# A phase mixer with a ternary feed-forward layer: the context's statistics behind the first of four product units, their spread behind the second, and a new first step

## The chip, the cores and the metric

The kernel runs on one core of one Trainium2 chip. The metric is the device time of one execution in microseconds, the median of several runs. The times before are 1537.38, 1531.16 and 1529.48 us.

## The reference

The input x has 16 sequences of 1024 positions with 256 features, in fp32.

```
h   = layernorm(x)
omega = h @ W_omega.T + b_omega
phi = cumsum(omega * exp(log_scale) / sqrt(position))
cm_real, cm_imag = h * cos(phi), h * sin(phi)
mem_real, mem_imag = cumsum(cm_real) / position, cumsum(cm_imag) / position
ret_real = mem_real * cos(phi) + mem_imag * sin(phi)
ret_imag = mem_imag * cos(phi) - mem_real * sin(phi)
context = concat(cm_real, cm_imag, ret_real, ret_imag)        # 1024 features
g   = gelu((layernorm(context) * gamma + beta) @ W1.T + b1)   # 512
x1  = x + h + g @ W2.T + b2
out = x1 + relu(layernorm(x1) @ T(F1).T + f_b1) @ T(F2).T + f_b2
```


## The kernel before

**Tiling.** The 16384 rows are 32 chunks of 512; two chunks make a sequence, and the second takes up the first one's sums by carries (`carry_phase`, `carry_imag`, `carry_real`). Features lie on the 128 partitions. Every product is made in fp16 from a high and a low part: `context_hi` on ScalarE writes the high part `ch`, `context_lo` on VectorE the difference `cl`, and so for the gelu's output (`gelu_hi`, `gelu_lo`), the relu's (`relu_hi`, `relu_lo`) and the two norms.

**Steps.** Each engine has a `step(s)`, run for s from -1 to 31, whose order is written out by hand. In one step four chunks are under way: `now` (s) is in its feed-forward layer, `nxt` (s+1) in the two mixer products, `ahead` (s+2) in phase, sums and context, `far` (s+3) in its first norm and omega; `before` (s-1) is stored. Engines meet by semaphores alone; a wait stands in front of the instruction that needs it, and all behind it on that engine wait too. In step -1 there is no `now`; in that step the weights for later products are turned too.

**TensorE** (L1033). `hidden(nxt, m)` (L955) for m from 0 to 3 is one of four product units: 24 matmuls of 512 columns into bank 4+m. `context_stats(nxt)` (L930) sums the context over its features with 72 one-column matmuls into bank 3, 64 from `ch` and `cl`, 8 from the sums of squares `q_hi` and `q_lo`. `spread(nxt)` (L949) turns the reciprocal deviations `crs` into a row on all partitions, in bank 2. The order is unit 0, unit 1, statistics, unit 2, spread, unit 3. Then come eight `ffn_in` (L970) into banks 4 to 7, with `omega(far)` (L915) behind the sixth, `ffn_out` (L991) three behind them into banks 0 and 1, and `mixer_out(nxt)` (L1005), the product with w2, into banks 4 and 5; then the last three `ffn_out`. In step -1 the groups of the second weight (`W2_GROUPS`, `turn_group`, `less_hi`) and the signs of the feed-forward weights (`SIGN_GROUPS`, `turn_signs`, L1102) are turned between the units: two groups ahead of the spread, the other six behind unit 3 and ahead of omega and `mixer_out`. Each group is copied out of its bank by ScalarE's `group_hi` (L831); two banks serve in turn. `ffn_in(0, 0)` waits for all of them.

**VectorE** (L1431). `fraction(ahead)`, `statistics_1(far)`, `lean_2(now)`, `modulate_imag(ahead)` (L1259), `sums_imag`, `gains_1(far)`, `modulate_real`, carry, `context_variance(nxt)` (L1335: five small instructions from bank 3 to `cve`), `second_lo(now)` (L1389), `memory_imag`, `sums_real`, `scale_hidden(nxt, 0..2)` (L1352: a unit times the spread row `rb`, out of its bank to z), `first_rows_lo(far)`, then the retrieval, `scale_hidden(nxt, 3)`, low parts and `relu_lo` among one another, `phase_turns(far)` (L1222), `mixer_residual(nxt)` (L1364), `phase_sums(far)` (L1232: two scans of 512), `statistics_2(nxt)`, `spread_2(nxt)`.

**ScalarE** (L737). `sums_hi(nxt)` (L654), `base_scaled(ahead)`, `whole_turns(ahead)`, `output(before)`, `sine`, `magnitude`, `normalise_2(now)`, `cosine`, `second_hi(now)`, `normalise_1(far)`, `modulated_hi(ahead)`, `first_rows_hi(far)`, `spread_out(nxt)` (L663: bank 2 to rb), three gelus, and the relus with the squares (`square_real`, `square_imag`) and casts of the retrieved parts among them.

**POOL** (L509). `base_bias(ahead)`, `inverse_std_2(now)` (L500, ve2 to rs2), `square_lo(nxt)` (L539), `inverse_std_1(far)` (L476), `x1_bias(now)`, `inverse_std_context(nxt)` (L504, cve to crs), `product_imag_sin(ahead)`, `retrieve(ahead)` (two accumulating DMAs, rr and ri), `output_sum(before)` (an accumulating DMA to the output), `square_sums(ahead)` (L531): behind `sqr_done`, `sqi_done` and `cl_done[3]` an addition of 1024 columns (L535), then one of 512 (L537). SyncE's queue transposes the norms' rows by DMA (turned2 for `ffn_in`, turned1 for omega), loads x and stores the output.

Of the kernel before, what the change touches and what calls it, by code (L numbers as in the profile page):

```python
# [43 lines left out]
def phase_mixer_layer(nc, x, w_omega, b_omega, log_scale, ln_gamma, ln_beta, w1, b1, w2, b2,  # L44
# [17 lines left out]
    with ctx:  # L62
# [140 lines left out]
        ps_rows_b = ps[:, 4:6, :].rearrange("p b (t d) -> p (b t) d", d=D)  # L203
        ps_rows_last = ps[:, 2:4, :].rearrange("p b (t d) -> p (b t) d", d=D)
# [137 lines left out]
        def need_sum(eng, s, c, back=0):  # L342

            wait(eng, s, c.counts.value(16, 16 * (c.more + 1 - back)))

# [121 lines left out]
        def _(pool):  # L467
# [41 lines left out]
            def step(s):  # L509
                before, now, nxt, ahead, far = s.chunk(-1), s.chunk(0), s.chunk(1), s.chunk(2), s.chunk(3)  # L510
                if ahead:
                    base_bias(ahead)
                if now:
                    inverse_std_2(now)
                if nxt:
                    square_lo(nxt, ahead)
                if far:
                    inverse_std_1(far)
                if now:
                    x1_bias(now)  # L520
                if nxt:
                    inverse_std_context(nxt)
                if ahead:
                    product_imag_sin(ahead)
                    retrieve(ahead)
                if before:
                    output_sum(before)
                if ahead:
                    square_sums(ahead)

            def square_sums(c):  # L531
                need(pool, sqr_done, c)
                need(pool, sqi_done, c)
                need(pool, cl_done[3], c)
                pool.tensor_tensor(sqr[:, :, :], sqr[:, :, :], turn[:, :, :], ALU.add).then_inc(q2_done, 1)  # L535
                need(pool, q2_done, c)
                pool.tensor_tensor(sqr[:, 0], sqr[:, 0], sqr[:, 1], ALU.add).then_inc(q_done, 1)  # L537

            def square_lo(c, after):  # L539
                if after:  # L540
                    need(pool, frac_done, after)
                need(pool, q_done, c)
                need(pool, qh_done, c)
                pool.tensor_tensor(q_lo, sqr[:, 0], q_hi, ALU.subtract).then_inc(ql_done, 1)
# [23 lines left out]
        def _(act):  # L568
# [36 lines left out]
            def whole_turns(c):  # L605
                need(act, y_done, c)
                need(act, q2_done, c, 1)
                act.activation(turn[:, :, :], ph[:, :, :], ACT.Identity, bias=rounder[:, 0:1]).then_inc(turn_done, 1)
# [128 lines left out]
            def step(s):  # L737
# [10 lines left out]
                if not now:  # L748
                    whole_turns(ahead)
                if nxt:  # L750
                    sums_hi(nxt)
# [18 lines left out]
                if now:  # L770
                    second_hi(now)
                if far:
                    normalise_1(far)
                if ahead:
                    modulated_hi(ahead)
                if far:
                    first_rows_hi(far)
                if nxt:
                    spread_out(nxt)
# [10 lines left out]
                if nxt and not now:  # L790
# [4 lines left out]
                    for n in SIGN_GROUPS[4:]:  # L795
                        group_hi(n)
# [104 lines left out]
            prepared(act)  # L901
# [3 lines left out]
        def _(pe):  # L905
# [49 lines left out]
            def hidden(c, m):  # L955
                if m < 2:
# [48 lines left out]
            def mixer_out(c, before):  # L1005
# [11 lines left out]
                rows = ps_rows_last if c.index == CHUNKS - 1 else ps_rows_b  # L1017
# [15 lines left out]
            def step(s):  # L1033
                now, nxt, ahead, far = s.chunk(0), s.chunk(1), s.chunk(2), s.chunk(3)
                if nxt:
                    hidden(nxt, 0)
                    if not now:
                        for n in W2_GROUPS:
                            turn_group(n)
                    hidden(nxt, 1)  # L1040
                    context_stats(nxt, ahead)
# [3 lines left out]
                if nxt:  # L1045
# [103 lines left out]
            prepared(pe)  # L1149
# [3 lines left out]
        def _(dve):  # L1153
# [210 lines left out]
            def mixer_residual(c):  # L1364
# [3 lines left out]
                dve.scalar_tensor_tensor(out=x1[:, c.b], in0=ps_rows_last if c.index == CHUNKS - 1 else ps_rows_b,  # L1368
# [62 lines left out]
            def step(s):  # L1431
# [18 lines left out]
                if ahead:  # L1450
                    modulate_imag(ahead)
                    sums_imag(ahead)
# [5 lines left out]
                if nxt:  # L1458
# [10 lines left out]
                if nxt:  # L1469
                    scale_hidden(nxt, 0)  # L1470
                    scale_hidden(nxt, 1)
                    scale_hidden(nxt, 2)
# [40 lines left out]
                if far:  # L1513
# [12 lines left out]
                if nxt:  # L1526
                    mixer_residual(nxt)
                if far:
# [107 lines left out]
            first_lo(second)  # L1636
            dve.wait_ge(p_spread, 3)
# [14 lines left out]
            context_lo(first, 1, cmi[:, :, :])  # L1652
            context_lo(first, 2, rr[:, :, :])
            context_lo(first, 3, ri[:, :, :])
            phase_turns(second)
            phase_sums(second)
            carry_phase(second)
# [31 lines left out]
```

## Time and profile before

| | |
|---|---|
| median of 3 runs | 1531.16 us (1529.48 to 1537.38) |
| profiled execution: its time | 1533.96 us |
| profiled execution: span | 1532.2 us |
| mean granted TensorE clock | 0.991 |
| TensorE matmuls busy | 1470.5 us, 96% |
| VectorE busy | 1438.2 us, 94% |
| ScalarE busy | 1253.4 us, 82% |
| POOL busy | 616.9 us, 40% |
| accumulating DMAs' queue (q0) | 83.37 MB, 34.3% of 16 engines |
| SyncE's and ScalarE's queue (q1) | 69.25 MB, 18.4% |

The span runs from the first to the last instruction. Busy is the union of an engine's instructions; issuing a DMA, waiting and registers don't count. A row of a timeline has its start, its length, the engine, the line of the kernel, the operation, output and inputs, the count of merged instructions and in brackets the idle time ahead with what ended it. Times are from the start of the span.

### The profile page before, as it was taken

The page shows a single profiled execution, that of the slowest core. Times are in us where ns is not written, and L with a number is a line of the kernel's source. Part 1 is how long each engine was busy: PE and PEld are TensorE (multiplying, and loading weights), DVE is VectorE, ACT ScalarE, POOL GpSimd, SP SyncE. Part 2 cuts the span into 40 slices and gives each one's busy share as a digit, 9 for nine tenths or more (in the row PEclk, how much of TensorE's full clock was granted, in tenths as well). Part 3 has the DMA queues.
Part 4 walks back from the last instruction along what each step waited for, and adds up shares of the span by engine and source line. Part 5 has one row for each costly group of instructions (what it writes and reads, how often), then busy time and mean ns, then how long its engine had stood idle before and what let it go on. Part 6 is the DMA issues. An engine that isn't in the chain of part 4 may idle for free.

```text
span 1532.2 us, 29929 instructions
## 1 busy us (share of the span) xinstructions
PE 1470.5 (96%) x10685; PEld 878.0 (57%) x10685; DVE 1438.2 (94%) x2325; ACT 1253.4 (82%) x1773; POOL 616.9 (40%) x393
## 2 busy tenths in 40 slices
PE   3779999999999999999999999999999999999998
PEld 2445566656555665555665655566565566555556
DVE  7999999999999999999999999999999999989954
ACT  6768888888988888988888898888888788888756
POOL 1333444433354443444444334444344444334331
PEclk9899999999999999999999999999999999999999
DMA  6325545555645655654555564455565455555452
GB/s 219 67 58 111 102 80 109 108 111 113 123 76 100 111 104 111 124 107 79 105 111 110 111 125 94 83 111 103 109 125 109 73 109 111 110 111 101 73 90 42
DMA packets 231427, 158.20 MB, mean 103 GB/s; under 512 B 138608, under 2 KB 221552, under 8 KB 231280
## 3 DMA queue, kind: packets, MB, share of 16 engines
q0 software_dynamic: 59376, 83.37, 34.3%
q1 hardware_dynamic: 170272, 69.25, 18.4%
q10 hardware_dynamic: 1632, 3.67, 0.7%
q8 instruction: 86, 1.41, 0.4%
q14 instruction: 61, 0.50, 0.1%
HBM read 24.13 MB, written 33.03 MB: 37 GB/s over the span
## 4 chain that ended last, share of the span: by engine, by line
DVE 35%; PE 24%; issue 14%; ACT 12%; POOL 7%; DMA 4%; SPq 2%; DVEq 1%; ACTq 0%; POOLq 0%
PE ps L966 11%; DVE arena L1332 5%; POOL sqr L535 4%; DVE arena L1400 4%; PE ps L1000 4%; PE ps L987 4%; POOL sqr L537 3%; PE ps L1021 3%; ACT xs L601 3%; DVE mr L1285 3%; ACT base L581 3%; DVE arena L1361 2%; DVE bn L1170 2%; DVE arena L1356 2%; DVE qb L1316 2%
## 5 line engine op out<-in xcount | busy, mean ns | idle before, releaser
L966 PE MATMUL ps<-arena,w_hi 128*128 128x512 f16 x2048 | 609.2, 379 | 3.0 <-DVE arena L1332 1.6
L966 PE MATMUL ps<-arena,w_lo 128*128 128x512 f16 x1024 | 388.3, 379 | 0.0
L966 PEld LDWEIGHTS ps<-arena,w_hi 128*128 128x128 f16 x2048 | 197.5, 98 | 224.2 <-issue 2.0
L987 PE MATMUL ps<-turned,fw_t 128*128 128x512 f16 x1024 | 250.6, 380 | 8.6 <-DMA turned<-rows 4.1
L1000 PE MATMUL ps<-fw_t,arena 128*128 128x256 f16 x2048 | 255.0, 273 | 1.9 <-DVE arena L1400 1.9
L1000 PEld LDWEIGHTS ps<-fw_t,arena 128*128 128x128 f16 x2048 | 197.8, 97 | 63.8 <-issue 16.7
L704 ACT ACTIVATE arena<-ps,relu_bias,relu_scale 128x512 f32<-128x512 f32 x256 | 197.0, 769 | 24.8 <-PE ps L987 24.4
L535 POOL TENSOR_TENSOR sqr<-sqr,turn 128x1024 f32<-128x1024 f32 x32 | 84.3, 2635 | 323.3 <-DVE arena L1332 323.3
L1400 DVE TENSOR_TENSOR arena<-arena 128x512 f16<-128x512 f32 x256 | 172.0, 681 | 19.5 <-ACT arena L713 17.5
L1021 PE MATMUL ps<-w_hi,arena 128*128 128x256 f16 x1024 | 172.9, 273 | 0.3 <-issue 0.3
L966 PEld LDWEIGHTS ps<-arena,w_lo 128*128 128x128 f16 x1024 | 100.0, 98 | 121.0
L987 PEld LDWEIGHTS ps<-turned,fw_t 128*128 128x128 f16 x1024 | 97.5, 98 | 109.4 <-DVE arena L1356 14.6
L713 ACT CAST arena<-arena 128x512 f16<-128x512 f32 x256 | 154.5, 615 | 4.3
L1021 PE MATMUL ps<-w_lo,arena 128*128 128x256 f16 x512 | 139.6, 273 | 0.0
L656 ACT CAST sqr<-sqr 128x512 f16<-128x512 f32 x32 | 19.8, 617 | 128.4 <-POOL sqr L537 128.4
L483 POOL DMA_DIRECT2D rr<-qa x32 | 29.5, 921 | 203.4 <-DVE rr L1322 203.4
L551 POOL TENSOR_TENSOR qa<-mi,sn 128x1024 f32<-128x1024 f32 x31 | 73.3, 2364 | 86.5 <-DVE mr L1285 86.5
L1021 PEld LDWEIGHTS ps<-w_hi,arena 128*128 128x128 f16 x1024 | 100.0, 98 | 12.6 <-issue 0.7
L670 ACT ACTIVATE arena<-arena,b_full,z_down 128x512 f32<-128x512 f32 x128 | 96.9, 804 | 10.9 <-DVE arena L1356 10.8
L1361 DVE SCALAR_TENSOR_TENSOR arena<-arena,up 128x512 f16<-128x512 f32 x128 | 92.0, 741 | 0.0
L1356 DVE TENSOR_TENSOR arena<-ps,rb 128x512 f32<-128x512 f32 x128 | 82.0, 682 | 8.9 <-ACT rb L666 6.2
L676 ACT ACTIVATE arena<-arena,up 128x512 f16<-128x512 f32 x128 | 88.1, 713 | 1.0
(189 smaller groups left out, 2850.4 us busy)
## 6 DMA issues: line engine op xcount, KB each, us to landing
x_rows<-in_L_attn_x SPq DMA_DIRECT2D x32, 512.0 KB, 6.5
rr<-qa POOLq DMA_DIRECT2D x32, 512.0 KB, 6.2
ri<-qb POOLq DMA_DIRECT2D x32, 512.0 KB, 9.0
base<-bias_rows POOLq DMA_DIRECT2D x32, 512.0 KB, 5.5
x<-bias_rows POOLq DMA_DIRECT2D x32, 512.0 KB, 5.5
out<-x SPq DMA_DIRECT2D x31, 512.0 KB, 7.6
out<-x POOLq DMA_DIRECT2D x31, 512.0 KB, 11.2
arena<-in_L_attn_W ACTq DMA_DIRECT2D x1, 2048.0 KB, 11.8
```

Source lines behind the costliest of these rows:

```text
L535: pool.tensor_tensor(sqr[:, :, :], sqr[:, :, :], turn[:, :, :], ALU.add).then_inc(q2_done, 1)
L670: act.activation(z[:, m], z[:, m], ACT.Gelu, scale=z_down[:, 0:1], bias=b1_full[:, m:m + 1])\
L676: act.activation(gh[:, m], z[:, m], ACT.Copy, scale=up[:, 3:4]).then_inc(gh_done[m], 1)
L704: act.activation(rf[:, m % SLOTS], ps[:, 4 + m % KE], ACT.Relu, scale=relu_scale[:, 0:1], bias=relu_bias[:, m:m + 1]).then_inc(relu_done, 1)
L713: act.copy(rh[:, m % SLOTS], rf[:, m % SLOTS]).then_inc(rh_done, 1)
L966: last = pe.matmul(ps[:, 4 + m], w[:, k, m * P:(m + 1) * P], a[:, c.b, k], start=(i == 0), stop=(i == len(passes) - 1))
L987: last = pe.matmul(ps[:, 4 + m % KE], fw1_t[:, k, m * P:(m + 1) * P], a[:, k], start=(i == 0), stop=(i == len(passes) - 1))
L1000: last = pe.matmul(ps_rows_a[:, j], a[:, m % SLOTS, j * P:(j + 1) * P], fw2_t[:, m], start=(m == 0 and j % 2 == 0 and a is rh), stop=(m == ...
L1021: last = pe.matmul(rows[:, j], a[:, m, j * P:(j + 1) * P], w[:, m], start=(i == 0), stop=(i == len(passes) - 1))
L1356: dve.tensor_tensor(z[:, m], ps[:, 4 + m], rb[:, :], ALU.mult).then_inc(z_done[m], 1)
L1361: dve.scalar_tensor_tensor(out=gl[:, m], in0=z[:, m], scalar=up[:, 3:4], in1=gh[:, m], op0=ALU.mult, op1=ALU.subtract).then_inc(gl_done[m], 1)
L1400: dve.tensor_tensor(rl[:, m % SLOTS], rf[:, m % SLOTS], rh[:, m % SLOTS], ALU.subtract)\
```

## The change

On TensorE, in every step with a `now`, `context_stats(nxt)` stands behind unit 0 and `spread(nxt)` behind unit 1. VectorE's `context_variance(nxt)` stands behind `modulate_imag(ahead)`, and `scale_hidden(nxt, 0)` and `(nxt, 1)` behind `second_lo(now)`. ScalarE's `spread_out(nxt)` stands behind `second_hi(now)`. On POOL `square_lo(nxt)` is first and waits for the phase sums in place of the fraction, `output_sum(before)` stands behind `inverse_std_2(now)`, and `inverse_std_context(nxt)` ahead of `x1_bias(now)`. The wide addition of `square_sums` is an accumulating DMA, issued ahead of the wait for `cl_done[3]`.

In the first step (no `now`) the four groups of signs of the second feed-forward weight leave the step: they are turned in step 0, two behind the statistics, two behind unit 1. `mixer_out(nxt)` stands ahead of omega, chunk 0 takes banks 6 and 7 for it, and chunk 1's units wait for `z_done` of their own bank (units 2 and 3 for `x1_done` too). VectorE's `gelu_lo` stand ahead of the signs, and `phase_turns(far)` behind the residual. Before the first step VectorE makes the last three low parts and the second chunk's phase sums ahead of the scales, and TensorE and ScalarE wait for the scales no longer or later. The diff, cut to its core:

```diff
         ps_rows_b = ps[:, 4:6, :].rearrange("p b (t d) -> p (b t) d", d=D)
+        ps_rows_first = ps[:, 6:8, :].rearrange("p b (t d) -> p (b t) d", d=D)
...
+        def mixer_rows(c):
+
+            if c.index == 0:
+                return ps_rows_first
+            return ps_rows_last if c.index == CHUNKS - 1 else ps_rows_b
...
             def step(s):
                 before, now, nxt, ahead, far = s.chunk(-1), s.chunk(0), s.chunk(1), s.chunk(2), s.chunk(3)
-                if ahead:
-                    base_bias(ahead)
-                if now:
-                    inverse_std_2(now)
                 if nxt:
                     square_lo(nxt, ahead)
+                if ahead:
+                    base_bias(ahead)
+                if now:
+                    inverse_std_2(now)
+                if before:
+                    output_sum(before)
                 if far:
                     inverse_std_1(far)
+                if nxt and now:
+                    inverse_std_context(nxt)
                 if now:
                     x1_bias(now)
-                if nxt:
+                if nxt and not now:
                     inverse_std_context(nxt)
                 if ahead:
                     product_imag_sin(ahead)
                     retrieve(ahead)
-                if before:
-                    output_sum(before)
...
             def square_sums(c):
                 need(pool, sqr_done, c)
                 need(pool, sqi_done, c)
+                pool.dma_start(sqr[:, :, :], turn[:, :, :], accum_op=ALU.add).then_inc(q2_done, 16)
+                need_sum(pool, q2_done, c)
                 need(pool, cl_done[3], c)
-                pool.tensor_tensor(sqr[:, :, :], sqr[:, :, :], turn[:, :, :], ALU.add).then_inc(q2_done, 1)
-                need(pool, q2_done, c)
                 pool.tensor_tensor(sqr[:, 0], sqr[:, 0], sqr[:, 1], ALU.add).then_inc(q_done, 1)
...
             def square_lo(c, after):
                 if after:
-                    need(pool, frac_done, after)
+                    need(pool, y_done, after)
...
                 if not now:
                     whole_turns(ahead)
+                    prepared(act)
...
+                if now and now.index == 0:
+                    for n in SIGN_GROUPS[4:6]:
+                        group_hi(n)
                 if now:
                     normalise_2(now)
                 if ahead:
                     cosine(ahead)
+                if now and now.index == 0:
+                    for n in SIGN_GROUPS[6:]:
+                        group_hi(n)
...
                 if now:
                     second_hi(now)
+                if nxt and now:
+                    spread_out(nxt)
...
             def hidden(c, m):
-                if m < 2:
+                if c.index == 1:
+                    need(pe, z_done[m], c, 1)
+                    if m >= 2:
+                        need(pe, x1_done, c, 1)
+                elif m < 2:
                     need(pe, x1_done, c, 1)
...
+                    if now:
+                        context_stats(nxt, ahead)
+                    if now and now.index == 0:
+                        for n in SIGN_GROUPS[4:6]:
+                            turn_signs(n)
                     hidden(nxt, 1)
-                    context_stats(nxt, ahead)
+                    if now and now.index == 0:
+                        for n in SIGN_GROUPS[6:]:
+                            turn_signs(n)
+                    if now:
+                        spread(nxt)
+                    else:
+                        context_stats(nxt, ahead)
...
-                    spread(nxt)
+                        spread(nxt)
                     hidden(nxt, 3)
                     if not now:
-                        for n in SIGN_GROUPS[2:]:
+                        for n in SIGN_GROUPS[2:4]:
                             turn_signs(n)
+                        mixer_out(nxt, now)
+                        omega(far)
+                        return
...
                     modulate_imag(ahead)
+                if nxt and now:
+                    context_variance(nxt)
+                if ahead:
                     sums_imag(ahead)
...
                 if now:
                     second_lo(now)
+                if nxt and now:
+                    scale_hidden(nxt, 0)
+                    scale_hidden(nxt, 1)
...
                 if nxt and not now:
+                    for m in range(KE):
+                        gelu_lo(nxt, m)
                     dve.wait_ge(p_fw2, 16)
                     dve.wait_ge(p_tern, 2)
                     signs(1, fw2_in, fw2_signs)
-                    for m in range(KE):
-                        gelu_lo(nxt, m)
...
             context_lo(first, 0, cmr[:, :, :])
             first_lo(second)
+            context_lo(first, 1, cmi[:, :, :])
+            context_lo(first, 2, rr[:, :, :])
+            context_lo(first, 3, ri[:, :, :])
+            phase_turns(second)
+            phase_sums(second)
+            carry_phase(second)
             dve.wait_ge(p_spread, 3)
...
```

## Rows read from the trace of the kernel before

**Rows 1.** Busy time of each engine in windows; columns: stretch, length, PE, PEld, DVE, ACT, POOL, clock, DMA share, GB/s
```profile
core 0: us, PE busy (x) PEld busy (x) DVE busy (x) ACT busy (x) POOL busy (x), PEclk, DMA share, GB/s
62.10:110.30 48.20, 39.02 (x315) 24.45 (x315) 44.49 (x57) 30.89 (x44) 20.32 (x12) 0.93 0.41 77
...
742.30:787.20 44.90, 44.90 (x331) 26.70 (x329) 44.30 (x73) 38.25 (x54) 19.43 (x13) 1.00 0.56 106
1330.50:1380.50 50.00, 46.53 (x331) 27.10 (x330) 44.30 (x70) 38.94 (x56) 20.73 (x13) 0.97 0.52 96
...
155.20:1425.30 1270.10, 1258.93 (x9186) 748.43 (x9184) 1233.84 (x1975) 1069.85 (x1512) 543.01 (x337) 1.00 0.56 105
...
94.00:100.80 6.80, 3.43 (x32) 3.20 (x33) 6.80 (x8) 3.02 (x5) 2.85 (x2) 0.51 0.92 183
```

**Rows 2.** Waits of TensorE from 155.2 to 1425.3: us in total, times, longest
```profile
PE ps L987 <- DMA turned<-rows: 4.1, 7, 1.0
PE ps L987 <- DVE arena L1356: 3.6, 10, 0.7
PE ps L926 <- DMA turned<-xs: 3.0, 1, 3.0
```

**Rows 3.** Timelines of DVE, POOL and PE around two ends of a step
```profile
784.74 1.28 DVE L1368 SCALAR_TENSOR_TENSOR x<-ps,h_down,base 128x1024 f32<-128x1024 f32 x1
785.94 4.30 DVE L1237 TENSOR_TENSOR_SCAN ph<-ones,ph_carry,ph 128x512 f32<-128x512 f32 x2
...
784.38 2.64 POOL L535 TENSOR_TENSOR sqr<-sqr,turn 128x1024 f32<-128x1024 f32 x1 [10.05 <-DVE arena L1332]
787.10 2.07 POOL L537 TENSOR_TENSOR sqr<-sqr 128x512 f32<-128x512 f32 x1
...
787.15 0.60 PE L966 MATMUL ps<-arena,w_hi 128*128 128x512 f16 x2
...
1379.28 2.61 DVE L1237 TENSOR_TENSOR_SCAN ph<-ones,ph 128x512 f32<-128x512 f32 x2
...
1378.42 1.27 POOL L537 TENSOR_TENSOR sqr<-sqr 128x512 f32<-128x512 f32 x1
```

**Rows 4.** DMA issues of the page (KB each, us to landing), then ACT's timeline
```profile
rr<-qa POOLq DMA_DIRECT2D x32, 512.0 KB, 6.2
ri<-qb POOLq DMA_DIRECT2D x32, 512.0 KB, 9.0
...
776.37 1.06 ACT L661 ACTIVATE turn<-mi 128x1024 f32<-128x1024 f32 x1
...
781.10 1.04 ACT L633 CAST arena<-ri 128x1024 f16<-128x1024 f32 x1 [1.04 <-DMA ri<-qb]
```

**Rows 5.** Spread and low part of the step from 787.15; the step from 1380.50; DMA issue
```profile
804.50 0.60 PE L952 MATMUL ps<-ident,crs 128*128 128x128 f32 x4
...
801.77 1.23 DVE L1392 TENSOR_TENSOR rows<-xs,rows 128x1024 f16<-128x1024 f32 x1
...
1387.39 1.22 DVE L1263 TENSOR_TENSOR cmi<-xf,sn 128x1024 f32<-128x1024 f32 x1
...
1384.28 1.95 POOL L502 TENSOR_TENSOR rs<-ve,minus_half 128x4 f32<-128x4 f32 x1 [0.36 <-DVE ve L1386]
...
L498 POOL DMA_DIRECT2D out<-x x31 | 50.0, 1612 | 4.4 <-ACT x L614 4.4
```

**Rows 6.** Timelines of the first step, and the w2 product of a later one (chain of waits)
```profile
84.66 0.65 PE L952 MATMUL ps<-ident,crs 128*128 128x128 f32 x4 [1.96 <-POOL crs L507]
...
97.37 0.29 PE L1108 MATMUL ps<-rows,arena 128*128 128x128 f16 x1 [4.16 <-DVE arena L1549]
...
110.30 0.61 PE L966 MATMUL ps<-arena,w_hi 128*128 128x512 f16 x2 [1.44 <-DVE x L1368]
...
97.23 2.73 DVE L1361 SCALAR_TENSOR_TENSOR arena<-arena,up 128x512 f16<-128x512 f32 x4
...
58.86 1.05 ACT L633 CAST arena<-ri 128x1024 f16<-128x1024 f32 x1 [1.74 <-DMA ri<-qb]
...
734.61 5.24 PE ps L1021 x48
```

More of the change, by code:

```diff
@@ L510, in step @@
                 before, now, nxt, ahead, far = s.chunk(-1), s.chunk(0), s.chunk(1), s.chunk(2), s.chunk(3)
+                if nxt:
+                    square_lo(nxt, ahead)
                 if ahead:
@@ L514, in step @@
                     inverse_std_2(now)
-                if nxt:
-                    square_lo(nxt, ahead)
+                if before:
+                    output_sum(before)
                 if far:
                     inverse_std_1(far)
+                if nxt and now:
+                    inverse_std_context(nxt)
                 if now:
                     x1_bias(now)
-                if nxt:
+                if nxt and not now:
                     inverse_std_context(nxt)
@@ L606, in whole_turns @@
                 need(act, y_done, c)
-                need(act, q2_done, c, 1)
+                need_sum(act, q2_done, c, 1)
                 act.activation(turn[:, :, :], ph[:, :, :], ACT.Identity, bias=rounder[:, 0:1]).then_inc(turn_done, 1)
@@ L777, in step @@
                     first_rows_hi(far)
+                if nxt and not now:
+                    spread_out(nxt)
                 if nxt:
-                    spread_out(nxt)
                     gelu(nxt, 0)
@@ L794, in step @@
                     gelu_hi(nxt, 3)
-                    for n in SIGN_GROUPS[4:]:
-                        group_hi(n)
                 if now:
@@ L900, in _ @@
             act.activation(idle_sine[:, :], half_pi[:, 0:1], ACT.Sin)
-            prepared(act)
             run(act, step, -1)
@@ L1016, in mixer_out @@
                     need(pe, csq_done, c)
-                rows = ps_rows_last if c.index == CHUNKS - 1 else ps_rows_b
+                rows = mixer_rows(c)
                 for j in range(NT):
@@ L1148, in _ @@
             omega(second)
-            prepared(pe)
+            pe.wait_ge(p_lo, len(W1_GROUPS))
             run(pe, step, -1)
@@ L1367, in mixer_residual @@
                 need_dma(dve, added, c, 2)
-                dve.scalar_tensor_tensor(out=x1[:, c.b], in0=ps_rows_last if c.index == CHUNKS - 1 else ps_rows_b,
+                dve.scalar_tensor_tensor(out=x1[:, c.b], in0=mixer_rows(c),
                                          scalar=h_down[:, 0:1], in1=base[:, c.b], op0=ALU.mult, op1=ALU.add).then_inc(x1_done, 1)
@@ L1457, in step @@
                     carry_imag(ahead)
-                if nxt:
+                if nxt and not now:
                     context_variance(nxt)
@@ L1468, in step @@
                     carry_real(ahead)
-                if nxt:
+                if nxt and not now:
                     scale_hidden(nxt, 0)
                     scale_hidden(nxt, 1)
+                if nxt:
                     scale_hidden(nxt, 2)
@@ L1512, in step @@
                     context_lo(ahead, 1, cmi[:, :, :])
-                if far:
+                if far and now:
                     phase_turns(far)
@@ L1527, in step @@
                     mixer_residual(nxt)
+                if far and not now:
+                    phase_turns(far)
                 if far:
@@ L1651, in _ @@
             dve.tensor_scalar(thr[:, :], thr[:, :], 0.5, None, ALU.mult).then_inc(p_thr, 1)
[L1652 to L1657, printed above, removed]
             prepared(dve)
```

## Prediction

> **What bounds the kernel now.** I read the waits first, then windows of whole steps, then timelines. A step is the stretch from one chunk's first product unit (`hidden(nxt, 0)`) to the next one's. In a clean step TensorE is busy for the whole window of 44.9 us and VectorE for 44.3 of it [rows 1]; TensorE's own work is 44.85 us, so no reordering makes a step shorter than that. From the third chunk's start (155.2) to the 31st's (1425.3) lie 28 steps in 1270.1 us [rows 1]; 28 x 44.85 is 1255.8, so **14.3 us** is what a better order can win there. The waits name it [rows 2]: `ffn_in` waits for the transposed second norm (4.1 us, 7 times) and for the scaled unit 3 to leave its bank (3.6 us, 10 times), and once the turned first norm came 3.0 us late. That one step took 50.0 us, at a granted clock of 0.97 [rows 1], so 5.1 us of the 14.3 is one accident. The first step is the other place: 39.0 us of TensorE work in 48.2 us [rows 1].
>
> So VectorE is a hair from being the bound, and what it delivers late are those two releases. Look at the end of a step [rows 3]: the residual starts at 784.74, exactly when TensorE's w2 product is done, and the two scans of the phase follow in 4.30 us, to 790.24, which is 3.1 us into the new step (787.15). While they run, POOL runs its two additions of squares (2.64 and 2.07 us). One step later in the trace the first addition came early: there POOL's second took 1.27 and the two scans 2.61 us. Two fp32 instructions thus cost one another's time here.
>
> **The change, part by part.** *The wide addition of squares (L535) becomes an accumulating DMA*, 32 times. Removed: 2.64 us of POOL, all of it beside VectorE. Added: an issue of about 0.9 us on POOL, half a megabyte on its queue. The nearest rows are the other two SBUF-to-SBUF accumulations: 6.2 us from issue to landing for rr, 9.0 for ri, which queues behind rr [rows 4]. The new one is issued when the imaginary square is ready (777.43, which is 35.1 us into the step that began at 742.30), queues behind ri (cast on landing at 781.10, 38.8 into it) and so lands 1.0 after that at best and 9.0 after its issue at worst: 39.8 to 44.1. I take 42, ri's landing plus the 3 us by which ri came later than rr. The narrow addition needs this and `cl_done[3]` (what releases L535 at 784.38, 42.1 in), so it runs from 42.1 to 43.4 and is over before the first scan starts (43.6). Both scans then take 1.2 us each instead of 2.15: **VectorE gets 1.9 us per step**. At the worst landing the narrow addition falls between the scans and 1.3 of the 1.9 goes. The Trainium skill ("DMA: Bandwidth & Descriptors", Anatomy of one DMA) prices such a DMA lower, at 2.0 us plus its bytes over 436 thousand, an estimate of 3.2 us. By it the copy would land at 38.3, always early, and the late rival below would have no chance. The trace does not agree: rr took 6.2 and ri 9.0.
>
> *The statistics go behind unit 0, the spread behind unit 1* (all steps but the first). TensorE's work is the same. Its spread moves from 17.35 into the step (804.50 [rows 5]) to 12.16. What must be ready by then is crs. Worked from the step where the scans were quick, which starts at 1380.50 [rows 5]: ve2 is done at 3.7 and POOL's rs2 ends at 5.7; now `output_sum` stands next (1.6 us to issue), to 7.3; rs1, 2.0 us like rs2, to 9.3; meanwhile VectorE ends `modulate_imag` (6.9 to 8.0) and the variance's five small instructions (0.8) at 8.8; crs is the same operation on as many numbers, 2.0, to **11.3**. The spread waits for nothing, by 0.9 us. With the bounds: the scans 1.3 us slower gives 12.6, a wait of 0.45; four POOL instructions each held up by 0.5 more would be 13.3.
>
> *What that pulls forward.* `second_lo` ended at 803.00, 15.85 into its step [rows 5], and now ends near 13.8, so the transposes for `ffn_in` start 2 us sooner, though the DMA that adds the bias to x1 now overlaps them by 2 to 3 us: I count 0.5 to 2 us of lead gained. Unit 3's scaling comes right behind its product, over 1 us sooner than `ffn_in` wants it. The turned first norm gets 2 us as well. From `relu_lo(0)` on VectorE is paced by TensorE and ScalarE as before, so the DMAs of rr and ri don't move. ScalarE idles for some 1.2 us ahead of the earlier `spread_out`; it is busy for 82% of the span and now gets its squares' sums 3 us sooner, so this is free. `output_sum` leaves the queue behind ri and goes where the queue was empty; the new DMA takes its slot there.
> Of the 14.3 us I count **-12**: all but a late DMA now and then (9.2 lost in small pieces, 5.1 in the accident, some 2 kept).
>
> *The ramp.* TensorE's first unit starts at 62.1, the edge of its window, behind the last low part; in front of that stand, on VectorE, the scales and two other low parts. With the scales moved behind, it starts right after ScalarE's cast of ri (58.86 to 59.91 [rows 6]), and at 1.2 us it ends at 61.1: -0.9. The second wait is the spread at 84.66 for crs (1.96 us); the scales now stand between the scans and `fraction`, as long as before: 0 to -2 us, I take -1.5 (it decides little, because more pauses follow). Then the w2 signs: TensorE waited 4.16 us for them at 97.37, and their 32 passes and the product `mixer_out` ran behind them. Granted clock in 94 to 100.8, from this wait on: 0.51 [rows 1], the lower level of 1.2 GHz; TensorE was busy for 3.43 us of it with these 32 passes. Now `gelu_lo` (2.7 us for four, from 97.23, behind the signs [rows 6]) stands ahead of the signs, and `mixer_out` (5.2 us [rows 6]) can start near 96 with the clock again low for part of it, say 6.9 us, then omega 2.6: chunk 1 starts at 105.2 (+-1.5) and not at 110.30 [rows 6], whose wait for the residual the new banks remove. The 32 passes come back in the next step at full clock, half of 3.43 or 1.7 us, and VectorE enters that step 3 us late, for which I take 0.5. **Ramp -3**, bounds -5 and +0.5. The tail is TensorE's own row of work: 0.
>
> Sum: 1533.96 for the profiled execution, of which 1532.2 is the span, -12 - 3 = 1519. Its accident (5.1) is likely absent from the median run (1531.16, 2.8 lower); taking that back in part, a changed run without accident gives 1516 to 1519. **I say 1518.**
>
> **Rivals.** *The copy lands late or the lead is not enough.* The squares' DMA at the worst bound makes the spread wait 0.45 us per step, or x1's bias keeps the transposes from gaining anything: a third to nearly all of the 12 comes back, 1522 to 1530. For it: ri already took 9.0 us where rr took 6.2 [rows 4], so the queue is not empty there. Against: `output_sum` ran in that very slot before and has left it. *The change does nothing that counts*: the pauses are the accidents of DMA and stay, the ramp gives 1 or 2: 1529 to 1533. Against it: the waits for unit 3 come in 10 of 28 steps and not by chance, since VectorE's place in the step is the same each time. *Slower, by the spread.* Decides from crs at 12.16 on; everything is one chain there (w2 product, residual, scans, ve2, rs2, the issue of `output_sum`, rs1, crs, spread, the next w2 product), so each step then grows by what crs is late. At 13.3 this is 1.15 x 29 = 33 us against the 15 won: 1549. For it: POOL got a third instruction into that chain. Against: 0.9 us of room by rows.
>
> **How the numbers follow.** Forecast 0.66 (own range 1512 to 1523), late copy 0.12, nothing 0.12, slower by the spread 0.10. Half a per cent, 7.7 us, is about what a measurement of this kernel can tell from no change, so faster begins below 1523.5. Faster 0.69 (the forecast and a quarter of the late copy), same 0.21 (the rest of it and nothing), slower 0.10. The range leaves out the slower rival and a little below: 1511 to 1531.
>
> **What would show it.** Right: both scans near 1.2 us with the narrow addition ended before them; the wait of ScalarE for the sums (L656) mostly gone; TensorE's waits at `ffn_in` under 2 us in total; chunk 1's first unit near 105; steps of 44.85. Wrong: a row of TensorE's spread waiting for POOL's crs in most steps, or the narrow addition still beside the scans, or the turned norms landing later than before.

## The result, and the profile after

The changed kernel took **1518.93 us** (median of 6 runs, 1518.09 to 1523.0), the kernel before 1532.16 beside it (6 runs, 1529.48 to 1537.38): ratio 0.9914, 95% interval 0.9892 to 0.9935. Faster by 0.9%, more than the half per cent that the prediction could tell from nothing; it said 1518. The profiled execution took 1518.09 us with a span of 1516.3, at a mean granted clock of 0.990, so 15.9 us of the profiled span are gone. Of all the executions timed here, two took more than twice as long as the others (3931.86 us of the kernel before, 4160.53 of the changed kernel with two parts put back); they stand in no ratio.

First the page: busy time of the engines, and the two DMA queues.

```profile
PE 1469.0 (97%) x10685; PEld 880.7 (58%) x10685; DVE 1425.8 (94%) x2325; ACT 1255.7 (83%) x1773; POOL 537.2 (35%) x393
...
q0 software_dynamic: 63984, 100.15, 40.7%
q1 hardware_dynamic: 170272, 69.25, 20.0%
...
rr<-qa POOLq DMA_DIRECT2D x32, 512.0 KB, 7.9
ri<-qb POOLq DMA_DIRECT2D x32, 512.0 KB, 8.7
sqr<-turn POOLq DMA_DIRECT2D x32, 512.0 KB, 6.0
...
out<-x POOLq DMA_DIRECT2D x31, 512.0 KB, 6.5
```

POOL lost 80 us of work, VectorE 12; the accumulating queue moves 16.8 MB more. The new copy lands 6.0 us after its issue, and the output's DMA, moved to a quieter place, 6.5 us after its own. Then windows of the changed kernel: the first step, the next, and the 28 steps from the third chunk's start.

```profile
61.15:104.85 43.70, 36.85 (x282) 21.94 (x283) 41.08 (x70) 29.44 (x43) 16.42 (x10) 0.92 0.51 97
104.85:153.50 48.65, 46.88 (x360) 28.54 (x361) 47.68 (x77) 40.51 (x61) 16.95 (x12) 1.00 0.57 99
153.50:1409.45 1255.95, 1255.87 (x9186) 749.36 (x9184) 1225.98 (x1976) 1072.10 (x1513) 470.47 (x336) 1.00 0.64 118
```

The third row answers to the one of 1270.10 us in [rows 1]: the same 28 steps in 1255.95 us, of which TensorE is busy for 1255.87. Of the 14.3 us, 14.2 are won. The chunk 2 that began at 155.16 begins at 153.50, so the ramp gave 1.7. Together 15.9; the tail is unchanged within 0.1. TensorE's waits of the whole span say the same: those of [rows 2] are gone, and what is left (four rows of it here) lies ahead of chunk 2 or in the tail.

```profile
PE ps L942 <- DVE turned L1244: 6.8, 2, 3.5
PE ps L1041 <- DVE arena L1395: 4.5, 1, 4.5
...
PE ps L968 <- POOL crs L514: 0.9, 1, 0.9
PE ps L1007 <- DVE arena L1390: 0.9, 1, 0.9
```

Now the end of a step and the chain into the next one, which starts at 736.67; VectorE's timeline, then POOL's, of the changed kernel (answers to [rows 3, 5]).

```profile
734.26 1.28 DVE L1402 SCALAR_TENSOR_TENSOR x<-ps,h_down,base 128x1024 f32<-128x1024 f32 x1
735.46 2.33 DVE L1271 TENSOR_TENSOR_SCAN ph<-ones,ph 128x512 f32<-128x512 f32 x2
737.89 1.16 DVE L1278 COPY ph_carry<-ph 128x2 f32<-128x2 f32 x1
...
746.04 2.34 DVE L1305 TENSOR_TENSOR_SCAN mi<-ones,cmi 128x512 f32<-128x512 f32 x2
...
749.70 1.22 DVE L1426 TENSOR_TENSOR rows<-xs,rows 128x1024 f16<-128x1024 f32 x1
...
756.40 2.77 DVE L1248 TENSOR_TENSOR xs<-qb,xs 128x1024 f16<-128x1024 f32 x1
...
727.49 0.85 POOL L543 DMA_DIRECT2D sqr<-turn  x1 [5.00 <-ACT turn L670]
733.88 1.58 POOL L546 TENSOR_TENSOR sqr<-sqr 128x512 f32<-128x512 f32 x1 [5.54 <-DVE arena L1366]
737.87 1.16 POOL L553 TENSOR_TENSOR sqr<-sqr 128x512 f16<-128x512 f32 x1 [2.41 <-DVE ph L1271]
...
741.13 1.95 POOL L509 TENSOR_TENSOR rs<-ve,minus_half 128x4 f32<-128x4 f32 x1 [0.85 <-DVE ve L1420]
743.05 1.29 POOL L505 DMA_DIRECT2D out<-x  x1
744.43 1.94 POOL L485 TENSOR_TENSOR rs<-ve,minus_half 128x4 f32<-128x4 f32 x1
746.35 1.72 POOL L514 TENSOR_TENSOR crs<-cve,minus_half 128x4 f32<-128x4 f32 x1
...
755.74 2.35 POOL L560 TENSOR_TENSOR qa<-mi,sn 128x1024 f32<-128x1024 f32 x1 [6.39 <-DVE mr L1319]
```

The narrow addition (L546) ends at 735.46, the instant the scans start, and both take 2.33 us where they took 4.30. From there the chain runs as predicted: rs2 done 6.4 into the step, `output_sum`, rs1, and crs at 11.4 (10.3 in every other step) against the spread at 12.16. Two things here the prediction did not have. One is L1248: 2.77 us, where the kernel before needed some 1.6 and an undisturbed one takes 1.2. It starts 0.66 us after POOL's product (L560) and ends 1.08 us after that does (758.09), in this step as in all 28. The other is L1278, the copy of two columns that carries the phase from one chunk of a sequence to the next. It took 0.17 us in the kernel before; now it starts right behind POOL's low part of the sums (L553), which POOL's new order puts there, and takes 1.16, until that ends. It runs in every second step, and that is the 1.1 us by which crs comes later there.

### The profile page after: what moved, and what is told of

Read it like the earlier page. It is cut to its first block, busy times and chain, and to the rows that moved or that the text cites. A ratio compares the mean times of both kernels' runs of the same rounds, so it can differ in the third digit from the quotient of the medians.

```text
span 1516.3 us, 29961 instructions
## 1 busy us (share of the span) xinstructions
PE 1469.0 (97%) x10685; PEld 880.7 (58%) x10685; DVE 1425.8 (94%) x2325; ACT 1255.7 (83%) x1773; POOL 537.2 (35%) x393
## 3 DMA queue, kind: packets, MB, share of 16 engines
q1 hardware_dynamic: 170272, 69.25, 20.0%
## 4 chain that ended last, share of the span: by engine, by line
PE 89%; DVE 5%; ACT 2%; issue 2%; DMA 1%; POOL 0%; DVEq 0%; ACTq 0%; POOLq 0%
PE ps L986 40%; PE ps L1020 15%; PE ps L1007 14%; PE ps L1041 11%; PE ps L942 5%; PE ps L955 3%; DMA ri<-qb 1%; PE ps L968 1%; DVE mr L1319 1%; DVE xs L1248 0%; DVE arena L1390 0%; PE ps L961 0%; DVE ph L1271 0%; DMA lscale<-in_L_attn_log_scale 0%; DVE mi L1305 0%
## 5 line engine op out<-in xcount | busy, mean ns | idle before, releaser
L1434 DVE TENSOR_TENSOR arena<-arena 128x512 f16<-128x512 f32 x256 | 172.8, 685 | 27.8 <-ACT arena L722 23.5
L560 POOL TENSOR_TENSOR qa<-mi,sn 128x1024 f32<-128x1024 f32 x31 | 72.9, 2352 | 201.9 <-DVE mr L1319 201.9
L546 POOL TENSOR_TENSOR sqr<-sqr 128x512 f32<-128x512 f32 x32 | 46.2, 1444 | 182.4 <-DMA sqr<-turn 100.2
L1248 DVE TENSOR_TENSOR xs<-qb,xs 128x1024 f16<-128x1024 f32 x30 | 83.5, 2783 | 0.0
## 6 DMA issues: line engine op xcount, KB each, us to landing
out<-x SPq DMA_DIRECT2D x31, 512.0 KB, 10.3
```

What stands on the lines that cost most here:

```text
L1248: dve.tensor_tensor(rows1[:, :, 1], xs, rows1[:, :, 0], ALU.subtract).then_inc(l1_done, 1)
L1434: dve.tensor_tensor(rl[:, m % SLOTS], rf[:, m % SLOTS], rh[:, m % SLOTS], ALU.subtract)\
```

## The experiments

Three questions: which part carries the gain, how near the change stands to its slower rival, and whether something is left in the first step. Every kernel was timed beside the one before on the same chip.

### Which part carries it

**The change with the wide addition back on POOL:**

```diff
-pool.dma_start(sqr[:, :, :], turn[:, :, :], accum_op=ALU.add).then_inc(q2_done, 16)
-need_sum(pool, q2_done, c)
 need(pool, cl_done[3], c)
+pool.tensor_tensor(sqr[:, :, :], sqr[:, :, :], turn[:, :, :], ALU.add).then_inc(q2_done, 1)
+need(pool, q2_done, c)
```

> The changed kernel with the wide addition of squares back on POOL behind the last low part; all else as changed. Theory (POOL's wide addition holds up the phase scans, and the spread behind unit 1 can only be met without it): both scans near 2.2 us again, so ve2 near 5.3 us into a step, then POOL's low part, bias DMA, rs2, output_sum and rs1 in a row, crs near 13.0 to 13.7, and TensorE's spread waits 0.8 to 1.5 us in each of 29 steps: 1542 to 1562 us. Rival (the new places of statistics and spread carry the gain, the DMA is a mere substitute): no wait at the spread, 1518 to 1524 us.

Measured 1568.19 us, ratio 1.0231 (1.0189 to 1.0273): slower than both kernels, a little past the range expected. First TensorE's waits of this kernel from 160 to 1425, then POOL's and VectorE's timelines around the start of one step (760.27) and TensorE's spread in it.

```profile
PE ps L968 <- POOL crs L514: 19.2, 26, 1.1
PE ps L1007 <- DVE arena L1390: 10.7, 24, 0.5
PE ps L942 <- DMA turned<-xs: 5.5, 2, 2.9
```

```profile
757.37 2.75 POOL L544 TENSOR_TENSOR sqr<-sqr,turn 128x1024 f32<-128x1024 f32 x1 [11.41 <-DVE arena L1366]
760.20 2.07 POOL L546 TENSOR_TENSOR sqr<-sqr 128x512 f32<-128x512 f32 x1
...
771.92 1.72 POOL L514 TENSOR_TENSOR crs<-cve,minus_half 128x4 f32<-128x4 f32 x1
...
759.05 4.30 DVE L1271 TENSOR_TENSOR_SCAN ph<-ones,ph 128x512 f32<-128x512 f32 x2
...
773.70 0.54 PE L968 MATMUL ps<-ident,crs 128*128 128x128 f32 x3 [1.10 <-POOL crs L514]
```

The scans are back at 4.30 us, crs is done 13.4 into the step and the spread waits for it in nearly all steps. This is the prediction's slower rival, complete. All of the change but the DMA is a loss of 33 us against the kernel before. Of it 31.8 lie in the 28 steps behind chunk 2's start, and 1.7 ahead of it.

**The kernel before with the wide addition as a DMA**, and nothing else (the edit above, the other way round).

> The kernel before with one change: the wide addition is an accumulating DMA. Statistics, spread and first step as before. Theory: the scans fall to about 1.25 us each, VectorE is some 1.9 us earlier in each step, unit 3 is scaled and the second norm's low part made that much sooner, and TensorE's waits at ffn_in in the steady steps fall under 2 us: 1519 to 1523 us, the gain without the ramp's. Rival (the places carry the gain): the waits at ffn_in stay, 1529 to 1533 us.

Measured 1526.28 us, ratio 0.9945 (0.9923 to 0.9967): between the two. The new DMA in this kernel's page, and its waits (the first for POOL, then TensorE from 160 to 1425) say why.

```profile
sqr<-turn POOLq DMA_DIRECT2D x32, 512.0 KB, 8.7
```

```profile
POOL sqr L537 <- DMA sqr<-turn: 235.1, 30, 9.4
...
PE ps L987 <- DMA turned<-rows: 3.8, 6, 1.0
PE ps L987 <- DVE arena L1356: 2.0, 4, 0.6
```

`output_sum` still stands right behind `retrieve` here, so its DMA is ahead of the squares' copy in the same queue. The copy lands 8.7 us after its issue (median), the narrow addition waits for it in 30 of 32 steps, and in 18 of the 28 steady steps one of the two scans runs beside that addition at 2.2 us.

**The kernel before with that DMA and POOL's new order** (`square_lo` first, waiting for the phase sums, and `output_sum` behind `inverse_std_2`), all places and the first step as before:

```diff
 if nxt:
     square_lo(nxt, ahead)
 if ahead:
     base_bias(ahead)
 if now:
     inverse_std_2(now)
+if before:
+    output_sum(before)
...
     retrieve(ahead)
-if before:
-    output_sum(before)
```

> The kernel before with the wide addition as a DMA and POOL's new order (the low part of the sums first, output_sum behind rs2); places of statistics and spread and the first step as before. Theory (the output's accumulating DMA must leave the slot ahead of the squares' copy, or the copy lands late): the narrow addition ends ahead of the first scan in nearly every step as in the changed kernel, steady steps of 44.85 us, 1518 to 1522 us. Rival (the new first step and the earlier spread hold a part of it): 1524 us or more.

Measured **1517.64 us** (1516.76 to 1518.44), ratio 0.9911 (0.9887 to 0.9935): the whole gain, and a hair below the range expected. Its page's copy, and its window from chunk 2 to chunk 30:

```profile
sqr<-turn POOLq DMA_DIRECT2D x32, 512.0 KB, 5.3
```

```profile
153.75:1409.65 1255.90, 1255.90 (x9187) 749.57 (x9185) 1184.34 (x1976) 1072.38 (x1514) 480.98 (x336) 1.00 0.63 118
```

No pause of TensorE in 28 steps, as in the changed kernel. VectorE is busy for 1184.3 us of them, in the changed kernel for 1226.0; the low part of the first norm takes 34.0 us of them here and 79.0 there (rows further down).

**The change with statistics and spread in their old places** (and all that belongs to them on VectorE, ScalarE and POOL; the DMA, POOL's order and the new first step kept):

```diff
-if now:
-    context_stats(nxt, ahead)
 ...
-if now:
-    spread(nxt)
-else:
-    context_stats(nxt, ahead)
+context_stats(nxt, ahead)
 hidden(nxt, 2)
...
+spread(nxt)
 hidden(nxt, 3)
```

> The changed kernel with statistics and spread back behind unit 1 and unit 2 on TensorE, and the five small instructions, the scalings of units 0 and 1, the copy of the spread row and crs back in their old places; DMA, POOL's other order and the first step as changed. Theory: steady steps of 44.85 us as in the changed kernel, 1517 to 1521 us. Rival (the places carry it): waits at ffn_in come back, 1527 to 1532 us.

Measured 1518.82 us (1517.84 to 1519.56), ratio 0.9906 (0.9879 to 0.9932): the same as the change. The move of statistics and spread, which gives the change its name, brings nothing.

**The kernel before with the new first step alone.**

> The kernel before with the new first step and the new order ahead of it alone; wide addition on POOL, POOL's order and all steady places as before. Theory: the ramp's 1.7 us of the traces (third chunk begins at 153.5 and not 155.2) and nothing else, 1529 to 1531 us. Rival (the shift of the first steps cures later waits too): 1524 us or less.

Measured 1533.55 us, ratio 1.0001 (0.998 to 1.0022). Chunk 1 starts at 107.79 instead of 110.30, but chunk 2 at 156.94 instead of 155.16. So the theory, which put the ramp's 1.7 us down to the new first step, is wrong: alone it starts chunk 2 later by 1.8. The DMA and POOL's order with the old first step (above) start it at 153.74, which is 1.4 of the 1.7.

**The kernel before without the wide addition.** The squares of the imaginary part are left out of the variance; POOL's first addition is gone and nothing takes its place.

> The kernel before without the wide addition at all: the squares of the imaginary part are left out of the context's variance. It bounds what its removal can give where no copy has to land. Theory (POOL's hold on the scans is the whole loss): narrow addition over before the first scan in every step, scans of 1.25 us, steady steps of 44.85: 1518 to 1522 us. Rival (part of the loss is the transposes' own and stays): 1524 to 1528 us.

Measured 1518.96 us (1518.33 to 1519.52), ratio 0.9921 (0.9892 to 0.995). Both scans take 1.2 us and the steady steps 44.85, with `output_sum` in its old place and no new DMA. So the pauses of [rows 2] came from POOL's addition beside the scans, and not from transfers as such.

### How near the slower rival is

**The change with `output_sum` back behind `retrieve`**, and then **the same with the old places** too.

> The changed kernel with output_sum back behind retrieve, ahead of the squares' DMA. Theory: the squares' copy queues behind the output's and lands 1 to 3 us later, so the narrow addition starts at -1 to +0.5 us of the step and one scan is 1 us longer in most steps; but rs1 and crs have lost the 1.3 to 1.6 us issue ahead of them, crs near 10 to 11, no wait at the spread; a few waits for the transposes at ffn_in: 1519 to 1525 us. Rival (the price is the same order in either place, nothing changes): 1518 to 1519 us.

> The changed kernel with two edits together: the statistics and the spread in their old places, and the output's DMA back behind the two retrieval DMAs, so that the squares' copy lands late. Beside the run that had the second edit alone (1546.93 us) it differs by the places alone. Theory, that the new places make a late copy dear because crs has 0.9 us of room there instead of 2: 1523 to 1529 us, TensorE's waits for crs and for the scaled unit 3 under 4 us together, while the narrow addition still ends after the first scan has begun in most steps. Rival, that the late copy itself (scans slowed, transposes late) costs 25 us wherever the statistics stand: 1540 to 1550 us with the wait for the scaled unit 3 in most steps.

Measured 1546.93 us (1544.98 to 1553.92), ratio 1.0111 (1.0075 to 1.0147), and 1527.74 us, ratio 0.9975 (0.9957 to 0.9993). The first missed both ranges, by over 20 us. The two differ by the places alone, and have the copy equally late (page of the one, then of the other):

```profile
sqr<-turn POOLq DMA_DIRECT2D x32, 512.0 KB, 9.3
```

```profile
sqr<-turn POOLq DMA_DIRECT2D x32, 512.0 KB, 9.1
```

So a late copy costs 9 us in the old places and 28 in the new ones, against the runs where it is early (1518.82 and 1518.93). VectorE's groups over these steps show one part of the reason: the low part of the first norm, with `output_sum` back (it is 79.0 us in the changed kernel too); with the old places as well; and in the kernel with the DMA and POOL's order alone.

```profile
L1248 DVE TENSOR_TENSOR xs<-qb,xs 128x1024 f16<-128x1024 f32 x28 | 79.1, 2827 | 0.0
```

```profile
L1239 DVE TENSOR_TENSOR xs<-qb,xs 128x1024 f16<-128x1024 f32 x28 | 44.6, 1592 | 0.0
```

```profile
L1214 DVE TENSOR_TENSOR xs<-qb,xs 128x1024 f16<-128x1024 f32 x28 | 34.0, 1216 | 0.0
```

In the old places three scalings stand between the real scan and this instruction, and POOL's L560, released by the scan, is over or nearly over when it comes. In the new places two of them have gone ahead, the instruction falls beside L560 and costs 1.2 us more in every step than it does with a late copy in the old places (1.6 more than undisturbed). Two instructions behind it comes the scaling of unit 3, whose release `ffn_in` wants some 25.6 us into the step: the changed kernel gives it at 24.8 and 25.4 by turns, the old places at 24.5. The other part is the spread, for which crs is ready 0.8 or 1.8 us ahead (old places: 2.1). When the scans lose 1 us both run out. With `output_sum` back the 28 steps take 28.5 us more than in the changed kernel: the spread's lateness (its start behind 12.16 into the step) adds up to 10.8 of them, one step with a late turned norm has 4.9, and the rest, some 13, comes behind the spread, where unit 3's release is waited for. TensorE's waits with `output_sum` back, from 155 to 1425:

```profile
PE ps L1007 <- DVE arena L1390: 11.0, 26, 0.5
PE ps L968 <- POOL crs L514: 7.0, 11, 1.1
PE ps L942 <- DMA turned<-xs: 2.6, 1, 2.6
```

**The change with one more power ahead of crs**, its result unused:

```diff
+pool.tensor_tensor(spare[:, :], cve[:, :], minus_half[:, :], ALU.pow)
 pool.tensor_tensor(crs[:, :], cve[:, :], minus_half[:, :], ALU.pow)
```

> The changed kernel with crs computed twice, first into a spare tile: one more POOL power of four numbers, 1 to 2 us, right ahead of crs. Theory (the spread behind unit 1 has 0.8 to 1.8 us of room, and every us beyond it is paid in every step): crs near 12.3 in even and 13.4 in odd steps against 12.16, TensorE waits 0.2 and 1.3 us at the spread: 1532 to 1550 us. Rival (POOL has room, it is busy for 35% only): 1518 to 1521 us.

Measured 1528.11 us (1524.89 to 1529.48), ratio 0.9972 (0.9953 to 0.999): 4 us below the theory's range, 9 above the changed kernel. A step that starts at 200.81; POOL's timeline, and TensorE's spread.

```profile
210.48 1.72 POOL L515 TENSOR_TENSOR spare<-cve,minus_half 128x4 f32<-128x4 f32 x1
212.17 1.14 POOL L516 TENSOR_TENSOR crs<-cve,minus_half 128x4 f32<-128x4 f32 x1
...
213.37 0.65 PE L970 MATMUL ps<-ident,crs 128*128 128x128 f32 x4 [0.24 <-POOL crs L516]
```

The insertion cost 1.1 us and not the 2.0 it was priced at, so crs comes at 11.5 and 12.5 by turns and at most every second step waits. The 28 steps take 7.5 us more than in the changed kernel (the spread's lateness is 6.1 of them), and chunk 1's takes 1.9 more. The threshold is where it was put: 11.5 waits for nothing, 12.5 does. The step took 45.30 us, 0.45 more, with only 0.24 shown as a wait, so rows of waits understate what a late release costs: the spread starts at 12.56 instead of 12.16.

### What is left in the first step

**The change with omega ahead of the w2 product in the first step, and unit 0 waiting for each part of the context only where it is read; then the kernel before with the DMA, POOL's order and that second edit; and the changed kernel once more beside them.**

```diff
-if m == 0:
-    for part in range(4):
-        need(pe, ch_done[part], c)
-        need(pe, cl_done[part], c)
 for i, (w, a, k) in enumerate(passes):
+    if m == 0 and i % 6 == 0:
+        need(pe, ch_done[k // 2], c)
+        need(pe, cl_done[k // 2], c)
```

> The changed kernel with two edits in the first step: omega stands ahead of the w2 product, and unit 0 waits for each part of the context only ahead of the products that read it. If TensorE's pauses in the first step set the end: chunk 1 starts 1 to 2.5 us sooner and chunk 2 as much, 1516 to 1518 us. Rival, that VectorE sets chunk 2's start and its own row of work is as long as before: chunk 1 starts sooner, chunk 2 at 153 to 154 us as in the changed kernel, 1518 to 1520 us.

> The kernel before with the wide addition as a DMA, POOL's new order, and unit 0 waiting for each part of the context only where it is read; statistics, spread and first step as before. The run of this without the third edit gave 1517.64 us. If a late part of the context ever holds unit 0: 1514 to 1517 us. Rival, that unit 0's parts are all there in the steady steps and VectorE sets the first step's length: 1517 to 1519 us, steps of 44.85 and chunk 2's start at 153.0 to 153.8 us.

> The changed kernel once more, timed beside the others of this call, so that they are compared with it on one chip and not only with the kernel before: 1517.5 to 1520 us. If the new places and the new first step were worth anything, the kernel with the DMA and POOL's order alone would be slower than this one by over 1 us; by the theory that the two carry the whole gain the two differ by under 1.5 us either way.

Measured 1522.01 us (1521.5 to 1523.91; ratio 0.9929, 0.9909 to 0.9949), **1516.0** (1515.45 to 1518.01; 0.9889, 0.9869 to 0.9908) and 1518.76 us (1518.43 to 1520.14; 0.9908, 0.9886 to 0.993). The first got worse, past both its ranges: omega, brought forward, waits 6.0 us for the transposed norm, which the w2 product had hidden (timeline of TensorE):

```profile
98.19 1.89 PE L942 MATMUL ps<-turned,wo_hi 128*128 128x512 f16 x4 [6.02 <-DMA turned<-xs]
```

The second is the best kernel of all, each of its 5 runs below each of the changed kernel's 5 beside it. Its chunks 0, 1 and 2 start 2.3 to 2.5 us sooner than without the edit (62.44, 108.87 and 153.74 there). Timeline of TensorE:

```profile
59.96 0.59 PE L965 MATMUL ps<-arena,w_hi 128*128 128x512 f16 x2
...
106.53 0.60 PE L965 MATMUL ps<-arena,w_hi 128*128 128x512 f16 x2 [1.44 <-DVE x L1367]
...
151.40 0.38 PE L965 MATMUL ps<-arena,w_hi 128*128 128x512 f16 x1
```

So a late part of the context did hold unit 0, but in the first step only. In the traces that is worth 2.3 us to the end; between the two medians, which come from different chips, it is 1.6.

## Why the prediction was right, point by point

**The sum.** Predicted -12 in the steady steps and -3 in the ramp, measured -14.2 and -1.7. The two errors, 2.2 and 1.3, have opposite signs, and the total is off by 1 us of 15.9. That it is so near is in part luck. The cause of the steady gain was right; the moved statistics, which the prediction also counted on, gave nothing.

**The squares' DMA: right.** The copy was put at 42 us into the step and the narrow addition between 42.1 and 43.4; it starts at 42.05 to 42.8 and mostly ends at the scans' start, 43.6. The scans fell from 4.30 to 2.33 us, about the 1.9 counted. Two kernels show that this alone wins the steady 14.2 (the wide addition left out, and the DMA with POOL's order), one that without it the rest loses. ScalarE's wait for the sums went from 128.4 to 38.2 us, as the text expected. By the Trainium skill ("DMA: Bandwidth & Descriptors", Anatomy of one DMA), an estimate of 3.2 us for such a DMA, the copy could never have been late; it took 5.3 to 6.0 us, and 8.7 to 9.3 with the output's DMA ahead of it, where it landed behind the first scan's start in 25 to 27 of 28 steps.

**"Some 2 kept": wrong.** The steady term left 2 us for a late DMA now and then. No steady step waits in the changed kernel, apart from one of 44.93. The accident of [rows 1] didn't come back in its profile; in those of other variants it did (TensorE waiting 2.6 us for the turned first norm with `output_sum` back, 3.7 with the first step alone, 5.5 in two waits with the addition on POOL), all of them with slow scans. That slow scans cause it is only argued.

**The moved statistics: the chain was right, the benefit was not there.** crs was worked out at 11.3 and came at 10.3 and 11.4 by turns. The later of the two holds the 1 us of the phase's copy beside POOL's low part, which the prediction had not seen; without it the room at the spread would be 1.8 us in every step (worked out, not tried). `second_lo` was to end near 13.8 and ends at 13.2 and 14.2. But the lead of 0.5 to 2 us that this was to give `ffn_in` isn't needed once the scans are quick: in the old places the steps are 44.85 too. And "unit 3's scaling comes right behind its product, over 1 us sooner than `ffn_in` wants it" is the step that failed: it comes at best 0.8 us sooner, in every second step some 0.2, once 0.1 late, and 0.3 to 0.8 later than in the old places. The prediction checked POOL's queue and the DMAs of everything it moved, but not what VectorE's next instruction then meets on POOL (L1248 beside L560, 1.2 us per step more than in the kernel before; L1278 beside L553, 1 us in every second).

**The output's DMA: a part that was undervalued.** "`output_sum` leaves the queue behind ri and goes where the queue was empty; the new DMA takes its slot" stands in the prediction as an aside, comes back as the argument against the late copy, and isn't given a price. It decides between 1518.93 and 1546.93 us.

**The ramp.** First unit 61.17 (said 61.1), `mixer_out` at 94.94 (near 96), chunk 1 at 104.86 (105.2): right. The step that failed is what comes back in the next one: 1.7 for the moved signs (1.8 measured) and 0.5 for a late VectorE, which was 2.0: 0.9 of waiting at the spread, 0.9 at unit 3's release, 0.2 in smaller pieces. These rows of TensorE in the changed kernel's step of chunk 1 are the two waits.

```profile
119.87 0.65 PE L968 MATMUL ps<-ident,crs 128*128 128x128 f32 x4 [0.90 <-POOL crs L514]
...
134.36 1.04 PE L1007 MATMUL ps<-turned,fw_t 128*128 128x512 f16 x4 [0.86 <-DVE arena L1390]
```

Chunk 2 starts at 153.50 with the new first step and at 153.74 with the old one: where TensorE is released sooner at chunk 1 it waits in the next step. So beside the DMA and POOL's order the new first step holds 0.2 us of the ramp's 1.7, and that its -3 came out as near as it did is luck. In the repeated run of the changed kernel chunk 1 came 1 us later (105.9) and chunk 2 at 153.8 all the same. That VectorE's row of work sets chunk 2's start behind the new first step is argued from this, not tried by itself. Behind the old one it doesn't: there the finer waits brought chunks 1 and 2 forward alike.

**The rivals.** "Nothing counts" is out. "Late copy" was put at 1522 to 1530: with the copy truly late that is what the old places give (1526.28, 1527.74), the new ones give 1547. "Slower by the spread" had the right place, threshold (12.16) and mechanism, at a price that left out the second wait behind it: 1568 for crs at 11.9 to 13.4, mostly near 13, where 1549 was said for 13.3. Its 28 steps take 46 us more than the changed kernel's, of which the spread's lateness is 23.5; the rest lies behind it, 0.4 to 0.6 us at unit 3's release in nearly every step and 8 in the two steps with a late turned norm.

## What to carry to other kernels

Where two engines block one another for whole instructions, look at which pairs of instructions meet, and again after every move: a reordering that is neutral for each queue can create a new pair and eat the slack that hides it. When an addition is handed to a DMA, the place of its neighbours in the same DMA queue decides as much as the DMA itself. Try the parts of a change alone: here two of them carry everything, and the kernel with only these and finer waits in the first unit is 2.8 us faster than the whole.

## What the runs showed of the hardware

An instruction of VectorE with two SBUF inputs does not run slower beside a POOL addition or product that began before it; it looks as if it stood still. L1248 starts at 756.40, POOL's L560 ends at 758.09, and L1248 ends at 759.17, 1.08 us after that; alone it takes 1.22. In the changed kernel this distance is 1.08 or 1.09 us in all 28 steps, wherever L1248 began, and it is the same for the slow scans of the kernel before. The Trainium skill ("SBUF — State Buffer", Who interferes with whom) says this: the pair of ports that VectorE and GpSimd share is an exclusive lock, held by whichever starts first for its whole instruction. The trace agrees for these pairs. It does not for POOL's powers of four numbers: L1305's two scans start at 746.04, while L485's power runs until 746.37 and L514's behind it, and they take 2.34 us together, as alone. Nor are two inputs needed: the copy L1278, which reads one SBUF tile, takes 1.16 us beside L553 in each of 14 steps, and 0.17 in the kernel before.

POOL's power of four numbers takes 1.72 to 1.95 us in the chain and 1.14 as the second of two. The same SyncE and ScalarE transfers (69.25 MB) took 18.4% of the DMA engines' time before and 20.0% after, with 16.8 MB more on the other queue; in the kernel with the DMA and POOL's order alone, which moves the same bytes, 18.7%. Why the whole change lengthens them stays open.
